# Attention layer with a one query per batch, Strassen products: the score weights' rows placed inside the product W21 x T3, and new orders for ScalarE and VectorE in phases 1 and 2

## The reference

```python
q = cond_1024[:, None, :] @ Wq.T + bq            # one query per batch, 2 batches, 16 heads of 32
k = x @ Wk.T + bk                                 # x: 2 x 2048 x 512, float32
v = x @ Wv.T + bv
q = q / sqrt(32)
scores = einsum('bhqd,bhkd->bhqk', q, k)[:, :, 0, :]
attn = clip(scores, 0.0, 1.0)                     # per head and position, no softmax
context = attn[..., None] * v                     # 2 x 2048 x 512
out = x + context @ Wo.T + bo
```

## Time and profile before

| | us |
|---|---|
| median of 3 runs | 186.14 |
| the three runs | 186.14, 186.15, 184.82 |
| the profiled execution, its own time | 185.97 |
| its span, first to last instruction | 184.2 |
| TensorE busy | 179.6 (97%) |
| VectorE busy | 170.3 (92%) |
| ScalarE busy | 115.6 (63%) |
| GpSimd busy | 14.3 (8%) |

### The profile page before, as it was taken

The page is one execution under the profiler, slowest core; times in us unless marked ns, Lnnn a source line. Parts: engine busy times, 40 slices in busy tenths (PEclk is TensorE's granted clock), DMA queues, the critical chain, the costliest instruction groups (busy, mean ns, idle before and its releaser), DMA issues.

```text
span 184.2 us, 2369 instructions
## 1 busy us (share of the span) xinstructions
PE 179.6 (97%) x795; PEld 145.9 (79%) x795; DVE 170.3 (92%) x188; ACT 115.6 (63%) x158; POOL 14.3 (8%) x20
## 2 busy tenths in 40 slices
PE   8999989999999999999999999999999999999993
PEld 2878758888878888888888888888888888888883
DVE  1799999999699999999999999999999999989963
ACT  4579964796587754765667764783486854766200
POOL 8000000000000020121000010111000001111000
PEclk9999999999999999999999999999999999999999
DMA  5999920027601116389468616399921206479695
GB/s 225 312 369 431 403 110 2 0 59 255 261 16 41 26 31 114 117 141 231 84 234 278 251 39 114 124 157 252 296 87 58 57 0 114 131 133 307 117 372 199
DMA packets 9355, 30.15 MB, mean 164 GB/s; under 512 B 1152, under 2 KB 1536, under 8 KB 9216
## 3 DMA queue, kind: packets, MB, share of 16 engines
q1 hardware_dynamic: 7616, 23.72, 35.6%
q0 software_dynamic: 1728, 6.29, 19.4%
HBM read 19.52 MB, written 8.39 MB: 152 GB/s over the span
## 4 chain that ended last, share of the span: by engine, by line
PE 85%; DVE 8%; DMA 3%; issue 1%; SPq 0%; ACT 0%; DVEq 0%
PE bank_y L354 9%; PE bank_y L358 9%; PE bank_y L356 9%; PE bank_x L354 8%; PE bank_x L358 8%; PE bank_x L356 8%; PE bank_z L354 6%; PE bank_z L358 6%; PE bank_z L356 6%; DVE form_lo L858 4%; PE score_bank L415 4%; PE score_bank L414 4%; DMA x_raw<-wv_t 3%; PE bank_x L429 3%; DVE work L1117 1%; DVE wv_lo L858 1%
## 5 line engine op out<-in xcount | busy, mean ns | idle before, releaser
L858 DVE TENSOR_TENSOR form_lo<-work,form_hi 128x1024 fp32r<-128x1024 f32 (+1 forms) x38 | 40.3, 1081 | 2.7 <-ACT form_hi L579 2.6
L579 ACT CAST form_hi<-work 128x1024 fp32r<-128x1024 f32 x28 | 29.1, 1052 | 20.7 <-PE score_bank L415 6.8
L614 ACT ACTIVATE work<-bank_y,const 128x512 f32<-128x512 f32 x30 | 19.7, 685 | 9.2 <-PE bank_y L358 9.2
L841 POOL DMA_DIRECT2D work<-x_t x12 | 10.5, 875 | 154.7 <-DVE work L891 147.9
L354 PE MATMUL bank_x<-form_hi,wo_hi 128*128 128x512 f32 x52 | 20.3, 391 | 0.0
L358 PE MATMUL bank_x<-form_hi,wo_lo 128*128 128x512 f32 x52 | 20.2, 389 | 0.0
L356 PE MATMUL bank_x<-form_lo,wo_hi 128*128 128x512 f32 x52 | 20.2, 389 | 0.0
L614 ACT ACTIVATE work<-bank_x,const 128x512 f32<-128x512 f32 x24 | 15.9, 684 | 6.3 <-PE bank_x L358 5.8
L880 DVE SCALAR_TENSOR_TENSOR work<-relu,work 128x1024 f32<-128x1024 f32 x16 | 19.4, 1220 | 0.3 <-ACT relu L643 0.3
L354 PE MATMUL bank_y<-form_hi,wv_hi 128*128 128x512 f32 x48 | 18.7, 389 | 0.0
L356 PE MATMUL bank_y<-form_lo,wv_hi 128*128 128x512 f32 x48 | 18.7, 389 | 0.0
(11 more groups left out here) (152 smaller groups left out, 386.7 us busy)
## 6 DMA issues: line engine op xcount, KB each, us to landing
x_raw<-x_t SPq DMA_DIRECT2D x16, 512.0 KB, 6.8
out_t<-work SPq DMA_DIRECT2D x14, 512.0 KB, 3.7
work<-x_t POOLq DMA_DIRECT2D x12, 512.0 KB, 5.3
score_others<-score_rows SPq DMA_DIRECT2D x16, 128.0 KB, 2.3
work<-first_t SPq DMA_DIRECT2D x2, 512.0 KB, 3.7
work<-wq_t SPq DMA_DIRECT2D x2, 512.0 KB, 9.1
work<-wk_t SPq DMA_DIRECT2D x2, 512.0 KB, 11.6
work<-wo_t SPq DMA_DIRECT2D x1, 1024.0 KB, 14.0
```

Of the source, the lines that this page charges most:

```text
L579: nc.scalar.copy(flat(form_hi, kind), raw(kind, phase)).then_inc(hi_ready[kind], 1)
L614: nc.scalar.activation(result_set(phase)[:, q, j * ROWS:(j + 1) * ROWS], of[:, j, :], ACT.Identity, bias=bias[:, tile:tile + 1], scale=sca ...
L841: pool.dma_start(output_set(s)[:, q, :], x_t[s, q], accum_op=ALU.add).then_inc(residual_added[q], 16)
L858: return nc.vector.tensor_tensor(to, of, hi.bitcast(F32), ALU.subtract)
```

## The change

The rows of the score weights are no longer made ahead of the product W21 x T3 but inside it, behind its first four matmuls (high x high), through a new argument `between` of `first_product`. Both the wait for q_parts and the eight matmuls move. ScalarE's and VectorE's instructions in phases 1 and 2 (and one pair of VectorE's in phase 3) are the same as before in another order. No instruction is added or taken away.

```diff
--- before.py
+++ after.py
@@ -415,7 +415,7 @@
                         mm = pe.matmul(bank, a_for_lo[:, b, at + k, :], form_lo[:, kind, k, :], start=False, stop=last)
                 return mm
 
-            def first_product(bank, form, kind, first, last):
+            def first_product(bank, form, kind, first, last, between=None):
 
 
                 terms = [(wv_hi, form_hi), (wv_hi, form_lo), (wv_lo, form_hi)]
@@ -431,6 +431,8 @@
                                            stop=last and w is terms[2][0] and y is terms[2][1] and k == 1)
                             if last and w is terms[2][0] and y is terms[2][1] and k == 1:
                                 mm.then_inc(first_done, 1)
+                    if between and w is terms[0][0] and y is terms[0][1]:
+                        between()
                 return mm
 
             def opening_products():
@@ -492,11 +494,12 @@
 
             first_product(banks[2], W12, B22, False, True)
 
-            pe.wait_ge(q_parts_ready, 1)
-            rows(a_rows_psum, q_parts, wk_hi_ready, wk_lo_ready).then_inc(a_rows_done, 1)
+            def score_weight_rows():
+                pe.wait_ge(q_parts_ready, 1)
+                rows(a_rows_psum, q_parts, wk_hi_ready, wk_lo_ready).then_inc(a_rows_done, 1)
 
             pe.wait_ge(first_out[Q11], 2)
-            first_product(banks[0], W21, T3, True, False).then_inc(w21_done, 1)
+            first_product(banks[0], W21, T3, True, False, between=score_weight_rows).then_inc(w21_done, 1)
 
             pe.wait_ge(q_ready, 2)
             pe.matmul(c_psum, const[:, C_SAME:C_SAME + P], bk_q[:, :, :], start=True, stop=True)
@@ -735,28 +738,28 @@
             wo_sum_part(S1, 0)
             wo_part(W22, 3)
             first_values(Q12, banks[2], 4)
+            wo_sum_part(S2, 1)
+            copy_a_rows()
             hi(T1, 1)
-            copy_a_rows()
-            wo_sum_part(S2, 1)
             wv_sum_part(S3, 3)
+            wo_sum_part(S3, 2)
+            copy_scores(0, 0)
             hi(T2, 1)
-            wo_sum_part(S3, 2)
+            hi(B11, 1)
             first_values(Q22, banks[0], 6)
-            hi(B11, 1)
             hi(B21, 1)
-            copy_scores(0, 0)
             hi(T4, 1)
             hi(T3, 1)
             copy_scores(0, 1)
+            copy_b11(1)
             hi(B22, 1)
-            copy_b11(1)
             relu_scores(0, 0)
-            wo_sum_part(S4, 3)
             copy_u2(1)
             hi(B11, 2)
+            wo_sum_part(S4, 3)
             relu_scores(0, 1)
+            copy_u3(1)
             hi(B21, 2)
-            copy_u3(1)
             copy_scores(1, 0)
             hi(T1, 2)
             copy_b11(2)
@@ -1162,29 +1165,29 @@
             scale_q()
             x_t1(1)
             scale_bk()
+            wo_sum(1)
             x_t3(1)
             wo_part(W11, 0)
             wo_part(W12, 1)
-            wo_sum(1)
-            lo(T1, 1)
+            wo_sum_part(S2, 1)
+            wo_sum(2)
             fill_a()
             split_a(0)
+            lo(T1, 1)
             x_t2(1)
+            wv_sum_part(S3, 3)
             sum_c()
-            wo_sum(2)
-            wv_sum_part(S3, 3)
+            wo_sum(3)
             lo(T2, 1)
+            lo(B11, 1)
             x_t4(1)
-            wo_sum_part(S2, 1)
-            lo(B11, 1)
             lo(B21, 1)
             lo(T4, 1)
             lo(T3, 1)
+            sum_scores(0, 0)
             lo(B22, 1)
-            sum_scores(0, 0)
-            wo_sum(3)
+            add_out11(1)
             context(0, Q11)
-            add_out11(1)
             sum_scores(0, 1)
             context(0, Q21)
             lo(B11, 2)
@@ -1210,8 +1213,8 @@
             lo(T4, 2)
             x_t1(3)
             lo(B21, 3)
+            add_out22(2)
             lo(T1, 3)
-            add_out22(2)
             x_t2(3)
             split_a(1)
             x_t3(3)
```

## The result

| | before | changed |
|---|---|---|
| median of 22 runs each | 185.62 us | 185.14 us |
| lowest, highest | 184.82, 186.16 | 184.6, 185.47 |
| profiled execution, own time | 185.97 | 185.33 |
| its span | 184.2 | 183.5 |

The ratio is 0.9974, 95% interval [0.9963, 0.9985]: 0.48 us faster (0.28 to 0.69), within the 1% that I called the same. The median before, over 22 runs, is 185.62 and not the 186.14 of the three runs shown; the changed kernel also scatters less (0.87 us from lowest to highest against 1.34).

A forecast was written before the change was run, and what follows sets the result against it. TensorE bounds the kernel, busy 179.6 of 184.2 us. 0.91 won at the rows less 0.21 at scores(0,0) is 0.70 us, giving 185.27 from the profiled 185.97, 185.44 on the median, called 185.4; range 184.1 to 186.4.

The forecast's parts named there:

- The one wait of 0.89 us and its restart: TensorE in front of the score weights' rows, until VectorE finishes q_parts: 1.04 us lost plus a restart of 0.12.
- 0.91 for the four matmuls: First four matmuls of W21 x T3 fill TensorE's wait before the rows, at 0.227 us each: 0.91 us gained.
- the rival by the 131 ns: TensorE packs tighter at the rows: the four matmuls fill only 0.52 us, gain 0.31, 185.8 us; chance 0.03.
- 0.21 given back at scores(0,0): VectorE's fill_a and split_a now hold TensorE at scores(0,0): a new wait of 0.09 us plus a restart of 0.12.
- The prediction's sum: 0.91 less 0.21 is 0.70 us; against the profiled execution's own 185.97, 185.27 us.
- The margin of 0.35 at B11(1): With copy_scores(0,0) ahead of hi(T2,1), lo(B11,1) ends 0.35 us before TensorE wants B11(1); 0.7 before; priced at nothing.
- the rival that ends slower: ScalarE's queue behind copy_scores(0,0) stalls TensorE at B11(1) if lo(B11,1) comes over 1.05 us later than worked out; chance 0.05.
- hi(B22,1): On ScalarE behind copy_b11(1): lo(B22,1) ends some 2 us later, near 45.25, with the product B22(1) 7.2 us behind 52.05.
- add_out11(1): On VectorE ahead of context(0,Q11), which ends at about 47.5 while hi(B11,2) starts at 48.8: free by 1.3 us.
- add_out22(2): On VectorE ahead of lo(T1,3): runs 1.1 us earlier than its former 76.19, B22(2) wanted it at 78.47; free.
- the tie at relu_scores(0,1): ScalarE's S4 part, 0.52 us, ahead of the relu: it ends at 51.0, VectorE wants it at 51.04; priced at nothing.
- the 0.05 slip of before: TensorE's slip in front of B11(2) at 52.05, from operands just in time: expected to stay, moving along 0.70 us earlier.

The follow-up runs named there:

- rows_only: The kernel before with TensorE's edit alone (rows behind the first four matmuls of W21 x T3), ScalarE's and VectorE's orders as before: 185.19 against 185.53 us, ratio 0.9977.
- before_q_early: The kernel before with scale_q ahead of wo_sum(0) on VectorE and ScalarE's S1 part behind first_values(Q12), TensorE's order unchanged: 185.09 against 185.62 us, ratio 0.9974.
- after_copy_late: The changed kernel with copy_scores(0,0) put back behind hi(B21,1) on ScalarE: 185.02 us against 185.62 of the kernel before, ratio 0.9975.
- change_again: The changed kernel, unchanged, run again on another opening: 185.19 us against 185.79 of the kernel before on that chip, ratio 0.9973.
- before_again: The kernel before, unchanged, run again as a control: 185.45 us against 185.79 of the same kernel on that chip, ratio 0.9992.

## Why the prediction was right, and where its size was off

**The place and the sign.** The one wait of 0.89 us and its restart were what could be won, four matmuls cover it, and nothing behind 52 is touched: confirmed by rows_only, by before_q_early, by the constant 133.9, and by VectorE's and TensorE's busy time behind 52 us, which is that of the earlier trace rows but for 0.01 (stage view of the changed kernel):

```profile
52.00:100.00 48.00, 48.00 (x213) 39.74 (x212) 47.62 (x48) 33.01 (x43) 3.60 (x4) 1.00 0.51 123
```

**0.91 for the four matmuls.** Their slot is 0.91 in the trace (24.32 to 25.23), so the 0.227 us per matmul held, and the rival by the 131 ns of the Trainium skill ("TensorE: Matmul & The Clock Gate", Back-to-back issue gap) falls.

**0.21 given back at scores(0,0).** Place right, size near: 0.16 in after_copy_late. In that opening B is V + 26.54; for the opening of the profile before the rule gives 24.78 + 26.56 = 51.34 and 51.34 + 133.92 = 185.26. The prediction's sum said 185.27. So the working was right for the execution on which it was made.

**The margin of 0.35 at B11(1).** lo(B11,1) ended at 37.04 + 1.22 = 38.26 and the product began at 38.66: 0.40. That copy_scores(0,0) ahead of hi(T2,1) costs nothing was right, and in the opening of change_again the margin was 0.41; the rival that ends slower never came near its point.

**hi(B22,1), add_out11(1), add_out22(2), the tie at relu_scores(0,1): free.** B11(2) begins 27.09 behind P with no wait on the way but the 0.05 slip of before, at 51.41, and what follows takes the same 133.92.

**The term that was mis-sized** is the gain itself, 0.70 where 0.48 came out. It was taken from one execution, whose V - P of 0.99 is the second largest of the thirteen openings (1.08, 0.99, 0.89). The size fits such an opening; in four of thirteen there is next to nothing to win, and the prediction took the gap for the same in all. It never asked how the two ends of the wait vary against each other: V hangs on a load, P on the opening's first matmuls. The means to ask were there: of three runs, one was 1.3 us faster than the others, more than the whole gap, and the prediction took it for a reading that is merely low. Under the two rules it would be an execution in which q_parts were in time and nothing was to be won: 184.82 - 133.92 puts B11(2) at 50.90, and before_again has it at 50.83. The range, 184.1 to 186.4, held the result; the reason was that those runs were in it, not that this was understood. Against the 186.14 of three runs the 185.14 measured looks like a full microsecond, and that is chance too: half of it is the median before, 185.62 over 22 runs. Luck is also in the forecast of 185.4, which is only 0.3 us off: it is made of a median before that was 0.52 too high and a gain that was 0.22 too large, and the two errors work against each other.

## What to carry to other kernels

A wait is the difference of two arrival times, and a profile shows one draw of it. Where the two ends hang on different causes, look at the scatter of the runs before the gap is put into a sum: covering it wins only in the executions in which it is open, and so it makes the kernel steadier as well (here the spread of 22 runs fell from 1.34 to 0.87 us). Look for the operation in front of the late end as well as for cover at the early one: here a swap of two lines on VectorE, with one on ScalarE moved out of its way, won as much as the whole change, and both together, with one more swap, most likely more than the change alone.

## What the runs showed of the hardware

ScalarE's first operation on one 512 KB load of the opening (wv_t), which waits for its landing, began between 6.88 and 8.08 us in thirteen executions of the same first loads, a scatter of 1.2 us that reaches V undamped 17 us later, as VectorE works without a gap of more than 0.12 us in between. The first matmuls scatter too, and move P by 0.9 us (23.62 to 24.47). From B11(2) to the end, 133.9 us with the 1.8 outside the span, the same thirteen executions agree within 0.05 us. The scatter of this kernel's time comes from its opening.
